# A transformer block on one core: two of four table instructions move from VectorE to GpSimd, and three pieces of side work are re-spaced

## The reference, cut to what matters

```python
mod = (silu(c) @ wmod).reshape(4, 6, 1, -1)          # sa, ca, ga, sb, cb, gb per sequence
h = layernorm(x) * (1 + ca) + sa
x = x + ga * causal_attention(h)                     # 16 heads, softmax over up to 1024 keys
h = layernorm(x) * (1 + cb) + sb
logits = h @ gate_w                                  # (tokens, 8)
top_logits, top_idx = top_k(logits, 2)               # two experts a token
combine = one_hot(top_idx) weighted by softmax(top_logits)
y_e = silu(h @ w1[e]) @ w2[e]
x = x + gb * sum_e combine[e] * y_e
```

## Time and profile before

| what | us |
|---|---|
| median of three runs | 1028.52 |
| the profiled execution, whole | 1026.26 |
| its span, first to last instruction | 1024.5 |
| PE busy | 910.5 (89%) |
| DVE busy | 738.2 (72%) |
| ACT busy | 577.4 (56%) |
| GpSimd busy | 347.4 (34%) |
| mean granted TensorE clock | 0.961 of full speed |

### The profile page before, as it was taken

How to read it: one execution, slowest core, us unless ns; L and a number is a source line. 1 busy time by engine, 2 the same in 40 slices (tenths; PEclk the granted TensorE clock), 3 DMA queues, 4 the chain that set the end, 5 groups by cost and what they waited for, 6 DMA issues and landing times.

```text
span 1024.5 us, 19379 instructions
## 1 busy us (share of the span) xinstructions
PE 910.5 (89%) x6174; PEld 535.3 (52%) x6174; DVE 738.2 (72%) x2346; ACT 577.4 (56%) x1257; POOL 347.4 (34%) x302
## 2 busy tenths in 40 slices
PE   5798899998899999989999888878699999999990
PEld 3443335333445334544443443423498899999880
DVE  8788766879666889757689767799337675444697
ACT  3235576676586667576666747557534534334452
POOL 1422021242424124325003433003177456655630
PEclk8899899999999999999999997989999999999995
DMA  8436436327316166253463565103413323222698
GB/s 275 123 63 125 62 77 140 62 39 145 66 27 138 41 101 139 66 74 89 73 117 100 124 112 170 36 23 111 137 47 124 99 68 104 78 78 68 207 297 293
DMA packets 83235, 110.61 MB, mean 108 GB/s; under 512 B 15930, under 2 KB 56434, under 8 KB 83138
## 3 DMA queue, kind: packets, MB, share of 16 engines
q1 hardware_dynamic: 75506, 89.45, 37.4%
q0 software_dynamic: 6816, 18.62, 5.8%
q10 hardware_dynamic: 816, 1.32, 0.4%
HBM read 69.42 MB, written 35.41 MB: 102 GB/s over the span
## 4 chain that ended last, share of the span: by engine, by line
PE 63%; DVE 14%; ACT 11%; issue 5%; POOL 3%; DMA 3%; SPq 1%; POOLq 0%; ACTq 0%; DVEq 0%
PE PO L1604 11%; PE PY L1481 9%; PE PS L1584 9%; PE PH L1481 9%; PE PM L1561 8%; ACT PR L979 5%; PE PHT L1688 3%; PE PX L1616 2%; PE PX L1530 2%; DVE MXF L1282 2%; PE PS L1588 2%; PE PX L1633 2%; DVE JK L1279 2%; PE PX L1539 1%; PE PX L1540 1%
## 5 line engine op out<-in xcount | busy, mean ns | idle before, releaser
L979 ACT ACTIVATE PR<-PS 128x512 f32<-128x512 f32 (+3 forms) x768 | 335.1, 497 | 165.0 <-PE PS L1588 128.4
L1279 DVE CUSTOM_DVE_ANT_0 JK<-PM,MK 128x128 bf16<-128x128 f32 (+3 forms) x512 | 239.6, 484 | 57.8 <-PE PM L1561 56.9
L1561 PE MATMUL PM<-QK 128*128 128x512 bf16 (+3 forms) x768 | 251.5, 336 | 26.9 <-DVE MXF L1282 15.6
L1584 PE MATMUL PS<-QK 128*128 128x512 bf16 (+3 forms) x768 | 250.7, 337 | 12.5 <-ACT PR L979 10.3
L1282 DVE TENSOR_REDUCE MXF<-PM 128x1 f32<-128x512 f32 x256 | 175.2, 684 | 76.5 <-PE PM L1561 74.8
L1584 PEld LDWEIGHTS PS<-QK 128*128 128x128 bf16 x768 | 75.2, 98 | 175.3 <-ACT PR L979 110.1
L1604 PE MATMUL PO<-PR,V 128*17 128x512 f32 (+3 forms) x1536 | 164.0, 500 | 0.0
L1561 PEld LDWEIGHTS PM<-QK 128*128 128x128 bf16 x768 | 76.0, 99 | 101.0 <-DVE MXF L1282 36.3
L1481 PE MATMUL PY<-W2S,HT 128*128 x852 | 120.2, 291 | 4.9 <-issue 4.3
L1037 ACT ACTIVATE HS<-PH 128x512 f32<-128x512 f32 x71 | 42.5, 598 | 135.4 <-PE PH L1481 133.3
L906 POOL DMA_INDIRECT XL<-H2D,TOK x71 | 78.7, 1109 | 113.6 <-DVE TE L1422 65.1
(11 more groups left out here) (263 smaller groups left out, 1201.6 us busy)
## 6 DMA issues: line engine op xcount, KB each, us to landing
QK<-SD SPq DMA_DIRECT2D x180, 128.0 KB
SD<-SP SPq DMA_DIRECT2D x42, 256.0 KB, 2.7
OP<-OS SPq DMA_DIRECT2D x64, 64.0 KB
LP<-LR SPq DMA_DIRECT2D x64, 64.0 KB, 2.3
W1S<-in_w SPq DMA_DIRECT2D x8, 512.0 KB, 5.8
W2S<-in_w SPq DMA_DIRECT2D x8, 512.0 KB, 4.8
X<-XA SPq DMA_DIRECT2D x3, 1024.0 KB, 9.1
H2D<-XA SPq DMA_DIRECT2D x3, 1024.0 KB, 4.9
```

Source lines behind the costliest of these rows:

```text
L979: eng.activation(PR[:, slot, i, c0:512], PS[m % 3][:, c0:512], ACT.Exp, scale=0.25).then_inc(S["exp"].sem, 1)
L1279: eng.tensor_tensor_reduce(JK[:, jk % 2, 0:w], PM[m % 3][:, 0:w], MK[:, 512 - w:512], 1.0, -3.0e38, ALU.add, ALU.max, MXA[:, mb, h, qt:qt ...
L1561: eng.matmul(PM[m % 3][:, 0:128 * (k1 - k0)], QK[:, r, h, 0, qt * 128:(qt + 1) * 128], QK[:, r, h, 1, k0 * 128:k1 * 128], start=True, stop ...
L1584: last = eng.matmul(PS[m % 3][:, c0:512], QK[:, r, h, 1, j * 128:(j + 1) * 128], QK[:, r, h, 0, 512 * f + c0:512 * f + 512], start=True, s ...
```

## The change

Four things are changed.

1. In a "hot" step DVE keeps parts 0 and 1 (OLO and OHI). The two halves of OHX go to GpSimd, as a tensor_tensor and a tensor_scalar behind each other, with a semaphore of their own, "both". The products of "tok" wait for it, and from the third step on OHI waits until GpSimd has read the buffer's last content. This holds for the eight steps of the first table and for the one step of the second.
2. The parts of `route(0)` are one tick apart in place of half a tick.
3. `table(0)` begins at tick 12 of window 14 in place of tick 6.
4. In window 13 the "stat2" steps of the third sequence come two a tick in place of four a tick, with two ticks in place of four between "rstd" and "h2", and "lgt" one tick later.

```diff
@@ table
-            places.append((at + 4 * rest * c, [(rest if n else 0, ("hot", s, c, n)) for n in range(4)]))
+            places.append((at + 4 * rest * c, [(rest if n else 0, ("hot", s, c, n)) for n in range(2)]))
@@ schedule
-    place(NG - 3, 4, ln2(B - 2, 4, 4))
+    place(NG - 3, 4, ln2(B - 2, 2, 2))
     for tp in range(4):
-        place(NG - 3, 15 + 2 * tp, logits(B - 2, tp))
-    place(NG - 2, 0, route(0, 0.5))
+        place(NG - 3, 16 + 2 * tp, logits(B - 2, tp))
+    place(NG - 2, 0, route(0, 1))
-    for k, parts in table(0, 6, 0.5, 2):
+    for k, parts in table(0, 12, 0.5, 2):
@@ gpsimd_program
+                elif kind == "hot" and a[2] == 1:
+                    s, c, _ = a
+                    t0, t1 = RANGE[s]
+                    j0, np = PAIRS[s] * c + 2 * NT * SEGS[s][0], PAIRS[s]
+                    _, high, both = [t[:, (c % 2) * (1 - s)] for t in HOTS[s]]
+                    po.wait_ge(*after("hot", *step))
+                    if c > 1:
+                        po.wait_ge(*after("px", "tok", s, c - 2))
+                    turn("both")
+                    eng.tensor_tensor(both[:, :, 1, :], high, IO[:, j0 + 1:j0 + 1 + np].unsqueeze(2).broadcast_to([128, np, t1 - t0]),
+                                      ALU.mult).then_inc(S["both"].sem, 1)
+                    turn("both")
+                    eng.tensor_scalar(both[:, :, 0, :], high, PI[:, 0:1], None, ALU.mult).then_inc(S["both"].sem, 1)
@@ vector_program
-                    dv.wait_ge(S["hot"], S["hot"].before[step])
@@ part 1
+                        if c > 1:
+                            dv.wait_ge(*after("both", "hot", s, c - 2, 1))
-                    elif part == 2:
-                        eng.tensor_scalar(both[:, :, 0, :], high, PI[:, 0:1], None, ALU.mult).then_inc(S["hot"].sem, 1)
-                    else:
-                        eng.tensor_tensor(both[:, :, 1, :], high, ...
@@ tensor_program, tok
-                    pe.wait_ge(*after("hot", "hot", s, c, 3))
+                    pe.wait_ge(*after("hot", "hot", s, c, 1))
+                    pe.wait_ge(*after("both", "hot", s, c, 1))
```

## The result

In twenty executions of each kernel on one chip the kernel before had a median of 1030.87 us and the changed one 1026.3 us; the ratio is 0.9961, with a 95% interval from 0.9943 to 0.9979, so 4.0 us faster (2.2 to 5.9). A second comparison gave 0.9962. The forecast was 6.1 us less, from a median of 1028.52, so 1022.4 us, with "faster by over 0.5%" as the likeliest outcome; it came out at 0.4%, within 0.5%. Of the 3.9 us between 1022.4 and 1026.3, 2.35 lie in the median that I started from and 1.5 in the change.

A forecast was written before the change was run, and what follows sets the result against it. DVE was taken as the bound over most of 600 to 700 us; 3.6 + 6.9 - 4.4 = 6.1 us less gives 1020.2 from the profiled 1026.26, or 1022.4 against the median 1028.52; the forecast's own range 1018 to 1026.5.

The forecast's parts named there:

- Window 13: Sums two a tick: 3.6 us less, from shorter waits for maxima and at the logits, and 1.6 from the clock.
- Window 14, ticks 0 to 13: Table work moves behind the maxima, leaving DVE 23.6 us; with 2 us added, 25.5 in place of 32.4, 6.9 less.
- the wait at `route` part 1: PE's 1.48 us wait there, in window 14, would fall under 0.3 us with the parts a tick apart.
- The table: Tick 14 to the eighth "tok": DVE's 1.30 plus GpSimd's 1.66 make 2.96 us a step, 4.4 us more in all.
- the sign that I had named for it: In the table, OLO or OHI would have durations well over 0.94 and 0.50 us.
- The rule that the prediction drew: DVE instructions with two SBUF inputs and GpSimd instructions reading SBUF never overlap; a table step costs both engines' sum.
- PE's waits at "tok": In the first table, these waits would name GpSimd's OHX and add up to 3 to 7 us.
- Behind the eighth "tok": To the first XT: no loss, DVE needing 20.6 of 21.2 us; its idle time falls from 6.79 to about 1.
- (b): Time only moved: window 13 gains 0, ticks 0 to 13 3.5, the table loses 4.4; about 1028, chance 0.22.
- (c): Slower through GpSimd's pair in the table: 1031 at 2.7 us a pair, 1037 at 3.5; chance 0.13.
- (a): DVE and GpSimd run side by side in the table, or the clock stays up: 1014 to 1018, chance 0.15.
- (d): Each table step's OHI also waits for GpSimd's pair of two steps before; no price of its own, no chance given.

The follow-up runs named there:

- the spread alone: Kernel before with only the third sequence's "stat2" sums two a tick and its logits a tick later: 1029.88 us, 0.9977.
- the swapped order: Changed kernel with GpSimd's two instructions of a table step reversed, the tensor_scalar ahead of the tensor_tensor: 1017.89 us, 0.9905 against the kernel before.
- the half move: Changed kernel with each hot step's tensor_scalar back on DVE and only the tensor_tensor on GpSimd: 1022.28 us, 0.9931 against the kernel before.
- The spacing without a move: Kernel before with changes 2 to 4, all four hot parts on DVE: 1021.8 us, 0.9895 against the kernel before; measured again, 1023.67 us, 0.9935.

## Why the prediction was right or wrong

**The step that failed** is the price and the owner of the wait in the table. The prediction took GpSimd's pair at 1.66 us with its tensor_scalar at 0.60, and put the wait of the two engines for one another on DVE, whose OLO and OHI were to be stretched. The tensor_scalar takes 1.12 us alone, the pair 2.13, and it is GpSimd that waits, 0.92 us a step. The sum shows little of it, because the errors nearly cancel: of the 3.9 us between 1022.4 and 1026.3 the starting point makes 2.35 and the stage 0.9, nearly all of it the term for ticks 0 to 13, which was 1.0 us too large; the other 0.6, between the stage and the medians, are too few to be told from noise.

**Window 13, 3.6 us less: right in size, by another way.** 3.3 us measured with the whole change, 3.2 with the spread alone. I had put 2.0 us of it on shorter waits and 1.6 on the clock. The waits for maxima did not shrink (3.8 us before, 4.9 after), nor did the 1.44 us at the logits, which moved to another instruction. That the clock gave the whole sum was luck as to size. The mean clock rose from 0.86 to 0.96, that is from 13.3 us at the lower level (twice 0.14 of 47.4) to 3.5, and where it fell again the gain was gone.

**Window 14, ticks 0 to 13, 6.9 us less: right, 1 us too large.** 5.9 us measured, to 24.0 us, and 5.9 with change 2 and 3 alone. DVE's work fell by 6.1 us as reckoned (27.18 to 21.04); its idle time is 3.0 us in place of the 2 that I added. I said that the wait at `route` part 1 would fall under 0.3 us; it is 0.89. A part of the 5.9 us is the clock's again, whose mean rose from 0.83 to 0.93: by these means 10.2 us of the stretch were at the lower level before and 3.4 after. With the later table the stretch took 24.0 us at 0.93 and 23.3 at 1.00, 0.7 us for 3.4 at the lower level, so as an estimate from these some 1.4 us are the clock's.

**The table, 4.4 us more: right in size, and the reason for it is the step that failed.** Measured is 44.6 against 40.65 from the last maximum to XT, 4.0 more, and a step of 3.06 us for the 2.96 forecast. But the sum was made as DVE's 1.30 plus GpSimd's 1.66, with DVE held back by GpSimd. From the third step on OLO and OHI were not held back; the sign that I had named for it, their durations well over 0.94 and 0.50 us, is absent but for one OLO of 1.12. GpSimd was held by DVE, 0.92 us in the tensor_scalar of each step from the fourth on (0.6 to 1.3 in the first three), and it was dearer than I took it: 0.75 + 1.12 + 0.26 of hand-overs is 2.13 us alone, not 1.66. The tensor_scalar of 1.12 us (forecast 0.60) was the mis-sized term, sized by an affine_select that has nothing of it but its one input; the tensor_tensor was 0.15 cheaper than forecast. The two errors nearly cancel, and that is luck: the pair came 0.47 us dearer, and DVE added 0.92 us to it in place of 1.30. Of the 4.0 us the later place alone makes 1.0 (41.6 against 40.65, at a clock of 1.00), the move to GpSimd 3.0. That the order of two instructions decides 0.63 us a step was not in the sum at all.

**What the earlier trace rows did show.** The rule that the prediction drew from the Trainium skill (SBUF — State Buffer, "Who interferes with whom") says that the first to start holds the other back entirely. The half that no row of before showed, GpSimd behind DVE, is in the changed kernel, where a tensor_scalar that starts 0.23 us into OLO is 0.92 us longer. "Entirely" doesn't hold for what runs when OLO starts: OLO and GpSimd's tensor_scalar lie beside each other for 0.8 us and more, in the kernel with the swapped order and in the one with the tensor_scalar alone on GpSimd, at a price of 0.1 to 0.5 us for both together. And the DVE instruction that waited for GpSimd's tensor_tensor in the half move had one SBUF tensor, a case that the prediction left out when it drew the rule for two inputs.

**PE's waits at "tok": the sum right, the name wrong.** Seven waits of 0.58 to 1.34 us add up to 6.8 us, in the forecast 3 to 7. The trace puts them down to OHI, long done, or to "issue", and not to OHX; that they are GpSimd's is seen from the times: its tensor_scalar ends at 683.70 (the 2.04 us that began at 681.66), and PE starts at 683.80. The waits by group, from 664 to 700 us:

```profile
PE PX L1652 <- DVE OHI L1382: 3.5, 3, 1.3
PE PX L1652 <- issue: 3.3, 4, 0.9
```

**Behind the eighth "tok", nothing: right, with a landmark misread.** The idle time went from 6.79 to 0.51 us, as forecast, and almost none is left to cover anything more. The prediction puts the eighth "tok" of the kernel before at 702.9 us; the first instruction behind it starts at 697.53, so it was at 697.2, and 702.9 is where the later table has it. The table's end came 6.3 us nearer to the first XT (26.9 to 20.65 us from the eighth addition), which are the six ticks of the edit, not 13.5. The sum isn't touched, since both stretches that it compares end 20 to 21 us ahead of XT. The dropped wait between OLO and OHI, put at under 0.1 us a step, is 0.11.

**The sum, and where the starting point stood.** The stage measured 5.2 us less, 0.9 short of the forecast 6.1 (window 13 was 0.3 short, ticks 0 to 13 1.0, and the table cost 0.4 less than forecast), and twenty executions say 4.6 by medians, 4.0 by the ratio. The larger error is the starting point. I added the 2.3 us by which the profiled execution lay under the median of three; against twenty it lay 4.6 us under. Its feed-forward part is the shortest of all that were profiled: 300.35 us, where the kernel with only the spread, with the same code there, took 310.0, and the other ten between 301.3 and 311.0. The difference is in pauses at a few tiles. Around the tile at 958 us, after:

```profile
PEld PH L1489 <- issue: 2.0, 1, 2.0
...
DVE YO L1463 <- remote: 1.7, 1, 1.7
```

The same tile in the kernel before:

```profile
PEld PH L1481 <- issue: 0.3, 1, 0.3
```

These pauses come and go from one execution to the next at the same few tiles; what they are isn't settled. A reader of the two profiles alone would have put them down to the change.

**Rivals.** (b), the time only moved, forecast about 1028 and so lies nearer to the measured 1026.3 than my 1022.4 does, and is wrong by its reasons: window 13 gave 3.3 us where it had none, and ticks 0 to 13 gave 5.9 where it had 3.5. (c) was right that the pair costs over 2.4 us in place, 3.06 a step with what holds it, and wrong on what follows: I had added DVE's own 1.30 us a step, which ran beside it. (a), side by side, is half true. (d) shows no cost: DVE's waits in the steps are for PE's "tok", not for GpSimd.

**A faster kernel.** Two variants lie below both kernels with intervals that don't touch the changed kernel's 0.9943 to 0.9979: the tensor_scalar alone on GpSimd, 0.9888 (to 0.9909), and the swapped order, 0.9905 (to 0.9932). The spacing without a move did so once (0.9895, to 0.9916) and not the second time (0.9935, to 0.9958), and the tensor_tensor alone doesn't (0.9931, to 0.9952). That the same program came out 0.4% apart in two comparisons is a warning for the first two, which were measured once, with six executions each. By the stage, which is free of the pauses but not of the clock in window 13, the tensor_scalar alone, the swapped order, the spacing alone and the tensor_tensor alone are at 107.4, 109.5, 109.8 (112.3 the second time) and 107.7 us. The cleanest comparison is the stretch in which they differ, from the last maximum to the eighth addition into TK, at a clock of 1.00: 19.4, 21.5, 21.3 and 20.5 us, and 24.2 in the changed kernel. The first, second and fourth of them:

```profile
672.30:691.70 19.40, 16.05 (x169) 7.43 (x171) 17.38 (x38) 12.57 (x33) 11.77 (x8) 1.00 0.09 27
673.20:694.70 21.50, 16.37 (x169) 7.42 (x171) 16.80 (x31) 12.99 (x33) 16.66 (x16) 1.00 0.10 24
670.40:690.90 20.50, 17.02 (x179) 7.84 (x175) 19.23 (x40) 13.16 (x35) 5.53 (x8) 1.00 0.09 23
```

The tensor_scalar alone on GpSimd is best by all three; the swapped order is better than the changed kernel, and not shown to be better than leaving everything on DVE.

## What to carry to other kernels

An instruction given to a second engine must be priced in place, with what the two engines hold of each other: in this kernel it paid to put the long one-input instruction where it is running when the other engine starts, not behind it, and to give the second engine only as much as fits into the first one's own time. Test a bundle of edits one by one: here the re-spacings made 8.1 us in the stage, and the move to GpSimd gave 2.9 of it back. When a variant drops a wait as well as moving work, price the wait on its own. A single profiled execution can be several us off its own median in code that nobody touched; before adding the distance, compare stretches between landmarks with a second execution.

## What the hardware showed that I had not expected

- On GpSimd a bf16 tensor_scalar with a per-partition operand takes 1.12 us for 336 elements, more than the tensor_tensor with two inputs, 0.75 us. On DVE it is the other way round, 0.31 against 0.51.
- Which engine waits depends on what is running: GpSimd's tensor_scalar behind OLO's start 2.04 us, ahead of it 1.12; DVE's OHI just behind GpSimd's tensor_tensor 1.05 us, and 0.50 where GpSimd runs its tensor_scalar.
- With the same program the mean granted clock in window 13 was 0.92 in one execution and 0.86 in another, and the stretch took 44.2 and 47.4 us: a gain that rests on the clock was there in eight of nine executions.
